# Cross attention outputs turned by DMA instead of TensorE, and the causal mask of nine of twelve self tiles copied by ScalarE

## Time and profile before

| | |
|---|---|
| median of 3 runs | 1791.77 us (1790.55 to 1792.18) |
| profiled execution, own time | 1792.66 us |
| its span | 1791.0 us |
| granted TensorE clock | 0.99 |
| PE busy | 1673.0 us, 93% of the span |
| DVE, ACT, POOL busy | 68%, 62%, 40% |
| one iteration (steady) | 107.1 us |

### The profile page before, as it was taken

The page is one execution under the profiler, slowest core; times in us unless marked ns, Lnnn a source line. Parts: engine busy times, 40 slices in busy tenths (PEclk is TensorE's granted clock), DMA queues, the critical chain, the costliest instruction groups (busy, mean ns, idle before and its releaser), DMA issues.

```text
span 1791.0 us, 34372 instructions
## 1 busy us (share of the span) xinstructions
PE 1673.0 (93%) x12306; PEld 1012.3 (57%) x12306; DVE 1209.0 (68%) x1920; ACT 1102.5 (62%) x1715; POOL 709.2 (40%) x964
## 2 busy tenths in 40 slices
PE   4879999999999999999999999999999999999988
PEld 1445555556555565555656555565655656555655
DVE  4568485685848768485675848668585776848673
ACT  4455665756567465665756567575666756567474
POOL 2251433534334452433534234452433535244320
PEclk9969999999999999999999999999999999999999
DMA  7363342734335363343735335373343635434320
GB/s 184 50 100 50 66 71 38 116 48 77 64 57 86 48 104 60 64 68 45 110 48 81 65 58 81 48 109 58 61 68 49 105 48 84 66 59 65 49 49 13
DMA packets 88720, 124.10 MB, mean 69 GB/s; under 512 B 10577, under 2 KB 56722, under 8 KB 88434
## 3 DMA queue, kind: packets, MB, share of 16 engines
q1 hardware_dynamic: 85570, 114.86, 41.0%
q0 software_dynamic: 2352, 8.26, 1.4%
q10 hardware_dynamic: 768, 0.57, 0.1%
HBM read 21.42 MB, written 8.39 MB: 17 GB/s over the span
## 4 chain that ended last, share of the span: by engine, by line
PE 67%; DVE 9%; POOL 8%; ACT 5%; DMA 5%; issue 5%; ACTq 0%; SPq 0%; DVEq 0%; POOLq 0%
PE o_pair L1392 12%; PE small L1482 8%; DVE negmax L956 6%; PE score L1353 6%; PE small L1223 5%; DMA Q<-negT 4%; PE small L1405 4%; PE small L1239 3%; PE o_pair L1223 3%; PE score L1330 3%; PE small L1516 2%; PE score L1276 2%; POOL q1p L555 2%; POOL q1f L540 2%; PE score L1359 1%
## 5 line engine op out<-in xcount | busy, mean ns | idle before, releaser
L716 ACT ACTIVATE P<-score 128x1024 f32<-128x1024 f32 x448 | 446.9, 1027 | 109.2 <-PE score L1330 50.7
L956 DVE TENSOR_REDUCE negmax<-score 128x4 f32<-128x1024 f32 (+1 forms) x384 | 460.1, 1219 | 29.7 <-PE score L1311 20.4
L978 DVE TENSOR_TENSOR P<-P,cross_bound 128x1024 f32<-128x1024 f32 x192 | 234.0, 1248 | 78.6 <-ACT P L716 78.4
L1392 PE MATMUL o_pair<-P,V 128*32 128x256 f32 (+1 forms) x4096 | 283.1, 363 | 2.4 <-DVE P L978 2.4
L764 ACT ACTIVATE score<-cross_q 128x1024 f32<-128x1024 bf16 x192 | 196.6, 1024 | 45.5 <-DVE negmax L956 44.1
L1353 PE MATMUL score<-Q,K 99*128 99x256 bf16 x1024 | 156.4, 275 | 17.2 <-ACT P L716 16.2
L1392 PEld LDWEIGHTS o_pair<-P,V 128*32 128x32 f32 x4096 | 86.2, 108 | 133.4 <-issue 79.9
L1516 PE MATMUL small<-xnT,w 128*128 128x256 f32 x600 | 156.7, 379 | 0.0
L516 POOL TENSOR_TENSOR x<-x,ffn 128x1024 f32<-128x1024 f32 x15 | 33.0, 2197 | 294.3 <-DVE negmax L956 294.3
L1353 PEld LDWEIGHTS score<-Q,K 99*128 99x128 bf16 x1024 | 84.4, 98 | 108.4 <-ACT P L716 56.2
L1311 PE MATMUL score<-K,Q 96*128 96x256 bf16 x768 | 119.6, 279 | 19.4 <-ACT score L764 15.5
(11 more groups left out here) (192 smaller groups left out, 3222.3 us busy)
## 6 DMA issues: line engine op xcount, KB each, us to landing
K<-k2p SPq DMA_DIRECT2D x96, 256.0 KB, 6.7
Q<-q2p SPq DMA_DIRECT2D x192, 128.0 KB, 4.0
Q<-q1p SPq DMA_DIRECT2D x90, 256.0 KB, 6.0
x_in<-in_x SPq DMA_DIRECT2D x16, 512.0 KB, 5.6
ctxT<-in_ctx SPq DMA_DIRECT2D x16, 512.0 KB, 5.3
k2f<-q1f SPq DMA_DIRECT2D x32, 256.0 KB, 5.3
out_y<-x POOLq DMA_DIRECT2D x15, 512.0 KB, 3.5
K<-k1p SPq DMA_DIRECT2D x90, 64.0 KB, 3.6
```

The lines of the kernel that those rows point to most:

```text
L716: A.activation(P[:, t % 4, :], score[b][:, :, :], ACT.Exp, scale=SCALE).then_inc(score_free[b], 1)
L956: V.tensor_reduce(negmax[:, k, h:h + 1024 // w], s.rearrange("p (h w) -> p h w", w=w), AX.X, ALU.max, negate=True).then_inc(score_free[b], 1)
L978: V.tensor_tensor(p, p, cross_bound[:, t % 2, :].unsqueeze(1).broadcast_to([128, 4, SEQ]), ALU.min).then_inc(probs_masked[1], 1)
L1392: last = T.matmul(o_ps[ob][32 * j:32 * j + 32, SEQ * gg + q0:SEQ * gg + SEQ], v, p, start=s == 0, stop=end, tile_position=(0, 32 * j), ski ...
```

## The change

Five things are changed together.

- **Cross outputs.** V2 gets its values and ones in alternate columns, so the values of an output are in the even rows of `o_sb` and the sums in the odd rows. For each of the four units SP moves 64 even rows into `inT` (128 KB) and one row of sums per head into `sums2` (`put_outputs2`). After row maximum 3 DVE takes the reciprocal of all sums (32 x 256), SP spreads these over 128 partitions by four DMAs from 8 partitions each (`put_inverses2`), POOL multiplies (`over_sums`, two of 128 x 512), and PE's `out2` reads `inT`. PE's `unit_turn` and `heads_turned` for the cross attention, DVE's `normalise` and ACT's two copies of turned outputs go. The final group keeps the old way.
- **Causal mask.** Self tiles take three buffers in turn (`o_pair` is the third). Tiles 0 to 2 keep their mask matmuls; for tiles 3 to 11 ACT copies the mask in first (`self_premask`) and PE waits for that copy.
- **v2.** Both halves are computed in the self scores, the evictions move from DVE to ACT, and the value bias is folded into `bo2` once, ahead of the loop. `out2_0` and `out2_1` stand before and after self tile 11.
- **k2.** The rest of its second half moves from DVE to a copy on ACT (`keys_full`) and a subtraction on POOL (`keys_rest`).
- **SP.** `put_neg(st, 1, 1)` goes ahead of the last parts of q1 and k1 and of the load of x; part 1 of k2 goes behind `put_neg(st, 0, 1)`.

The diff, cut to its core (row lengths as in the source; the hunks stand in the order of the file: banks, SP, POOL, ACT, DVE, PE):

```diff
-    attention = (["k2_0"] + p("m2T_1", "o2t0", "o2t1", "o2t2", "o2t3")
-                 + ["v2_0", "k2_1", "m1T_0"] + p("oT2_0", "oT2_1") + p("out2_0", "out2_1")
-                 + ["v2_1", "m1T_1", "o1t0", "o1t1", "oT1_0", "o1t2"])
+    attention = (["k2_0"] + p("m2T_1") + ["v2_0", "k2_1", "v2_1", "m1T_0"] + p("out2_0", "out2_1")
+                 + ["m1T_1", "o1t0", "o1t1", "oT1_0", "o1t2"])
...
+            def put_outputs2(g, u):
+
+                bank, before = o_bank(1, g, u)
+                b, gp = u // 2, u % 2
+                sp.wait_ge(o_free[bank], before + 1)
+                sp.dma_start(inT[64 * gp:64 * gp + 64, :, SEQ * b:SEQ * b + SEQ],
+                             o_sb[0:128:2, u % 2, :].rearrange("p (c q) -> p c q", c=NC)).then_inc(o2_moved[u % 2], 16)
+                sp.dma_start(sums2[8 * u:8 * u + 8, :], o_sb[1:128:32, u % 2, :]).then_inc(o2_moved[u % 2], 16)
...
+            def put_inverses2(g):
+
+                sp.wait_ge(inverse2_ready, g + 1)
+                for b in range(GB):
+                    for c in range(NC):
+                        sp.dma_start(over_sum[:, c, SEQ * b:SEQ * b + SEQ],
+                                     inverse2[16 * b + c:16 * b + 16:2, :].unsqueeze(1).broadcast_to([8, HD, SEQ])
+                                     ).then_inc(inverse2_moved[b], 16)
...
+                if prev:
+                    put_neg(st, 1, 1)
+                    put_part("q1", 2, i)
+                    put_part("k1", 2, i)
...
                     sp.wait_ge(xn_ready[0], i + 1)
                     sp.wait_ge(x1b_ready, i + 1)
                     sp.dma_start(x_in[:, :, :], x_v[i + 1]).then_inc(x_loaded, 16)
                 if prev:
-                    put_neg(st, 1, 1)
+                    for u in range(UNITS):
+                        put_outputs2(i - 1, u)
+                    put_inverses2(i - 1)
                 put_neg(st, 0, 0)
-                for n in range(2):
+                put_part("k2", 0, i)
+                put_neg(st, 0, 1)
+                for n in range(1, 3):
                     put_part("k2", n, i)
-                put_neg(st, 0, 1)
-                put_part("k2", 2, i)
                 for b in range(GB):
                     for n in range(3):
...
                 if nxt:
                     put_part("k1", 0, i + 1)
-                    for n in range(1, 3):
-                        put_part("q1", n, i + 1)
-                        put_part("k1", n, i + 1)
+                    put_part("q1", 1, i + 1)
+                    put_part("k1", 1, i + 1)
...
+            G.memset(V2[:, :, :, :], 1.0).then_inc(made, 1)
...
+            def over_sums(g, b):
+
+                for n in range(2):
+                    pool.wait_ge(o2_moved[n], 32 * (UNITS // 2) * (g + 1))
+                pool.wait_ge(inverse2_moved[b], 16 * NC * (g + 1))
+                at = slice(SEQ * b, SEQ * b + SEQ)
+                G.tensor_tensor(inT[:, :, at], inT[:, :, at], over_sum[:, :, at], ALU.mult).then_inc(o2_whole, 1)
...
+            def keys_rest(st, g):
+
+                pool.wait_ge(small_free[st.bank("k2_1")], st.this("k2_1"))
+                G.tensor_tensor(k2f[:, 1, :], k2f[:, 1, :], k2p[:, 0, 1, :], ALU.subtract).then_inc(rest1["k2"], 1)
...
                 cut_third(0, i, 0)
                 if nxt:
                     inverse_root(0, i + 1)
-                if prev:
+                keys_rest(st, i)
+                if prev:
+                    for b in range(GB):
+                        over_sums(i - 1, b)
                     add_bias2(i - 1)
...
                 bk = st.bank(f"k2_{c}")
-                act.wait_ge(small_free[bk], st.this(f"k2_{c}"))
+                A.activation(k2f[:, c, :], small[bk][:, :], ACT.Identity,
+                             bias=bk2[:, c:c + 1]).then_inc(small_free[bk], 1)
+
+            def values2(st, r):
+
+                bk = st.bank(f"v2_{r}")
+                act.wait_ge(small_full[bk], st.this(f"v2_{r}"))
+                A.activation(V2[:, 2 * r:2 * r + 2, :, 0:32:2],
+                             small[bk][:, :].rearrange("p (k h n) -> p k h n", k=2, n=HD),
+                             ACT.Copy).then_inc(small_free[bk], 1)
...
+            def keys_second(st, g, c):
+
+                bk = st.bank(f"k2_{c}")
+                if c == 0:
+                    act.wait_ge(small_free[bk], st.this(f"k2_{c}"))
+                else:
+                    act.wait_ge(rest1["k2"], g + 1)
                 A.activation(k2p[:, 1, c, :], k2f[:, c, :], ACT.Copy).then_inc(part2["k2"], 1)
...
-                    if u >= 2:
+                    if u >= 2 and a == 1 and not last:
+                        act.wait_ge(o2_moved[u % 2], 32 * (g * (UNITS // 2) + u // 2))
+                    elif u >= 2:
                         name = f"o{a + 1}t{u - 2}"
                         act.wait_ge(small_full[st.bank(name)], st.before(name) + 1)
                     A.activation(o_sb[:, u % 2, :], o_ps[b], ACT.Copy).then_inc(o_free[b], 1)
...
+            def self_premask(g, t):
+
+                n, before = self_tile(g, t)
+                act.wait_ge(score_free[n], before)
+                if t % 6 < 4:
+                    A.activation(bufs[n][:, :, :].rearrange("p c (j k) -> p (c j) k", j=2),
+                                 causal_q[:, :].unsqueeze(1).broadcast_to([128, 4, SEQ]),
+                                 ACT.Copy).then_inc(masked[n], 1)
+                else:
+                    A.activation(bufs[n][:, :, :].rearrange("p c (j k) -> p (c j) k", j=4),
+                                 causal_q[:, 128:256].unsqueeze(1).broadcast_to([128, 8, 128]),
+                                 ACT.Copy).then_inc(masked[n], 1)
...
+                self_premask(i, 3)
+                self_premask(i, 4)
+                values2(st, 0)
+                self_premask(i, 5)
+                self_premask(i, 6)
+                keys(st, 1)
+                keys_full(st, 1)
+                self_premask(i, 7)
                 cut_first(0, i, 0)
+                self_premask(i, 8)
                 cut_second(0, i, 0)
-                keys(st, 1)
-                keys_second(st, 0)
+                self_premask(i, 9)
+                values2(st, 1)
+                self_premask(i, 10)
                 maxima(st, 0, 0)
-                if prev:
-                    turns(st, "oT2_", inT)
-                keys_second(st, 1)
+                self_premask(i, 11)
+                keys_second(st, i, 0)
+                keys_second(st, i, 1)
                 cut_first(0, i, 1)
                 cut_second(0, i, 1)
...
+                    if t in (9, 13) and i is None:
                         normalise(st, 1, t // 5 - 1, g)
...
-                    if prev and t in (1, 4):
-                        normalise(st, 1, 2 if t == 1 else 3, i - 1)
+                    if prev and t == 3:
+                        for n in range(2):
+                            dve.wait_ge(o2_moved[n], 32 * (UNITS // 2) * i)
+                        V.reciprocal(inverse2[:, :], sums2[:, :]).then_inc(inverse2_ready, 1)
                     if not prev and t == 2:
                         keys_rest(st, i, 0)
-                    if t == 5:
-                        values2(st, 0)
-                    if t == 7:
-                        keys_rest(st, i, 1)
...
-                values2(st, 1)
...
+                    by_pe = t < SELF_PE_MASKED
+                    if not by_pe:
+                        _, use = masked_use("S1", g, t)
+                        pe.wait_ge(masked[n], use + 1)
+                    elif n == 2:
+                        for ob in range(2):
+                            if positive(g * UNITS):
+                                pe.wait_ge(o_free[ob], g * UNITS)
+                    elif positive(before):
                         pe.wait_ge(score_free[n], before)
                     if s < 4:
                         for j in range(4):
...
+                            last = T.matmul(bufs[n][:, j // 2, SEQ * (j % 2):SEQ * (j % 2) + SEQ],
+                                            Q1[0:KROWS, 4 * s + j, SEQ * b + 128:SEQ * b + 256],
+                                            K1[0:KROWS, s, SEQ * b:SEQ * b + SEQ], start=by_pe and j % 2 == 0,
+                                            stop=not by_pe, skip_group_check=True)
...
+                    for c in range(2) if by_pe else ():
+                        last = T.matmul(bufs[n][:, c, :].rearrange("p (h k) -> p h k", h=2)[:, :, 128:256],
+                                        identb[:, :], again(causal_q[:, 128:256], 2), start=False, stop=True,
+                                        skip_group_check=True)
                     last.then_inc(score_full[n], 1)
...
-                    if t == 1 and a == 0:
-                        tokens(st, "v2", ctxT, wv2, 1)
...
-                    if t == TPU[a] * (u + 1) + LAG + 2 and 0 <= u < UNITS - 1 and (a, u) != (0, 2):
```

(54 more changed lines are left out.)

111 lines of the change are left out of this document (60 added, 51 removed).

## The result

The kernel after takes 1873.89 us (median, 1869.23 to 1876.22), the kernel before beside it 1791.97: a ratio of 1.045 [1.044, 1.047]. It is 82 us slower where 42 us faster were forecast, and outside the range.

What follows compares the result with a forecast made beforehand. PE, busy 93% of the span, was taken as the bound, with DVE right behind in the self scores. 3.3 us gained less 0.5 gives 2.8 per iteration, 42 in 15: span 1791.0 to 1749, median forecast 1750 us, range 1722 to 1788.

Steps and rivals of the forecast that it cites:

- Outside: Prologue, iteration 0 and final piece: prologue nothing, at most 1 us; iteration 0 nothing, give or take 2 us.
- The rival on the slower side: Sums' round trip: reciprocal 4.1 and transfer spacing 2.0 us make self attend's tile 8 1.6 us later, 1816 us; chance 0.09.
- The walk of the loop: Timed path from last cross product to self attend's tile 8: 3.3 us gained at tile 6, 2.8 per iteration after allowance.
- After it nothing changes: Behind self attend's tile 6, the 3.3 us gained there was to stay; ACT is next late.
- the allowance: 0.5 us per iteration taken off for a dozen hand-overs counted at 0.1 us or nothing.
- Turns and masks: PE work removed per iteration: masks on nine tiles 2.9 us, unit turns 2.0, turn of all heads 1.1, together 6.0.
- Cross attend: PE-bound stage losing three turns: all later times come 1.5 us earlier; delayed q1 and k1 parts cost nothing.
- Reciprocal: DVE's one reciprocal of 256 elements in the self scores: 1.9 us, bounded by 0.43 and 4.1.
- Idles at tiles 7, 9, 10: Self scores: PE waits 1.4, 0.4 and 1.1 us in the chain of maximum, ACT mask copy and matmuls.
- Narrow transfers: Rival: inverse transfers reading 8 partitions take double, 2.0 us each, delaying POOL's second product; 1782 to 1792 us, chance 0.25.
- The forecast's line for being wrong: Signs: DVE waiting over 1 us for sums, POOL waiting for inverses' transfers, or PE idle over 3 us in self scores.
- The split: Per iteration, masks (2.9 us) and turns (2.0 + 1.1) counted together as 6.0 us of PE work, before waits.

Runs made afterwards that it cites:

- a_pad20: The kernel after with 20 small unused matmuls (40 TensorE instructions) added once ahead of iteration 0: 1765.29 us, ratio 0.984.
- a_pemask: The kernel after with 20 pads and all 12 self tiles masked by TensorE, cross outputs still by transfers: 1750.12 us, ratio 0.976.
- b_pad100: The kernel before with 100 small matmuls (200 TensorE instructions) added ahead of iteration 0: 1841.5 us, ratio 1.027.
- a_order: The kernel after with 20 pads and POOL's first product put ahead of k2's subtraction: 1739.64 us, ratio 0.971.
- a_bias: As a_order, with POOL's bias sums for out2 moved ahead of the first cut of the self maxima: 1746.98 us, ratio 0.975.
- a_bias_mix: As a_bias, with self tiles 7, 9 and 10 masked by TensorE instead of ScalarE: 1733.61 us, ratio 0.967.

## Why the prediction was wrong

**The step that failed** is in "Outside": "Prologue: two matmuls, a 128x256 sum on DVE (0.43 by the earlier trace rows) and a longer memset ... : nothing, at most 1 us", and with it the sum that counts only durations in the loop. What counted was how many instructions stand ahead of the loop: 25 fewer moved its start over a block's edge. a_pad20 gives the price, 1873.9 - 1765.3 = 109 us, or 8.4 us in each of 13 returns. It is a net price: in after the clock falls in the self scores in 3 of the 13 passes, in a_pad20 in 9, which makes up for part of the 9.3 us at the branch. Neither the sum nor a rival of the prediction had a place for where the loop starts. The rival on the slower side named a late inverse transfer and 1816 us; it isn't what happened.

**The walk of the loop** was right in its path and order up to tile 6 of the self attend, and wrong behind it. On a common clock, from self tile 0 (901.79 before, forecast 1.5 earlier; 677.99 in a_pad20):

```
                          before    forecast    a_pad20 at full clock
self attend's tile 0       20.85      21.3           20.48
tile 2                     23.56      22.7           22.28
tile 6                     28.89      27.1           26.73
```

With what the cross attend brings, a_pad20 is 2.4 + 2.2 = 4.6 us ahead at tile 6, where 3.3 were forecast. But the gain per iteration at full clock is 107.1 - 103.6 = 3.5 us: "After it nothing changes" was wrong by 1.1. A tile of the cross scores waits 1.08 us for ScalarE's mask copy where it waited 0.38, and the first tile of the next iteration starts 0.4 us later behind the work before it, with a wait for a negT transfer. The tile before, then both in a_pad20:

```profile
970.05 0.61 PE L1311 MATMUL score<-K,Q 96*128 96x256 bf16 x4 [0.38 <-ACT score L764]
```

```profile
744.79 0.61 PE L1415 MATMUL score<-K,Q 96*128 96x256 bf16 x4 [1.08 <-ACT score L852]
762.22 0.61 PE L1457 MATMUL score<-Q,K 99*128 99x256 bf16 x4 [0.24 <-DMA Q<-negT]
```

So 3.5 us lies near the forecast's 3.3 (2.8 after the allowance) in part by luck: two errors stand against each other. Step by step:

- *Turns and masks:* TensorE's busy time per iteration falls by 103.04 - 97.61 = 5.4 us of 6.0. In a_pemask, with the turns gone and the masks back, it is 99.82: 3.2 us for the turns (3.1 forecast), and so 2.2 for the masks (2.9 forecast).
- *Cross attend:* shorter by 21.81 - (677.99 - 658.63) = 2.4 us, not 1.5; a wait of 1.17 us for ScalarE's exponential at its third tile (884.53 us in the kernel before) is gone as well, which the prediction had no term for.
- *Reciprocal:* 1.73 us by the row of after below, 1.9 forecast. This was the unknown with the widest bounds, and the nearest row's slope gave it.

```profile
L1224 DVE RECIPROCAL inverse<-sums 32x256 f32<-32x256 f32 x15 | 25.9, 1730 | 0.0
```

- *Idles at tiles 7, 9, 10:* 1.07, 0.28, 0.85 against 1.4, 0.4, 1.1; before out2 0.75 against 0.9. Names and order right.
- *Narrow transfers (rival, 0.25):* the condition was half met. In a_pad20 the four are issued from 1001.70 on, each shows eight semaphore updates where out_y's transfer shows sixteen, and the last updates come at 1004.84, 1006.26, 1007.47 and 1008.57: 1.24 us apart, between the 0.98 taken and the rival's 2.0. POOL's second product starts at 1008.9, so no one waits. The Trainium skill, "DMA: Bandwidth & Descriptors" (Why a DMA increments its semaphore by 16 and not by 1), would have eight engines carry such a copy; the eight updates agree, the doubled price, which the prediction took with it, doesn't. (That rival's sum has a slip: 3.3 less 2.9 us leaves 0.4 us per iteration, not 0.7.)
- *What the walk lacked even at its own task:* idle time was priced at its own length. In 9 of 13 iterations the clock fell behind 2.95 us of it, which cost 1.7 more. The forecast's line for being wrong, "more than 3 us of PE idle in the self scores", lies on just that amount, but no term followed from it.
- *The split:* the prediction summed masks (2.9) and turns (3.1) and then took off the waits from both. The runs show that the waits at tiles 7, 9 and 10 go with ScalarE's masks, which are worth 0.3 us at full clock or less than nothing.

With the loop in place the change gives 1765 us: within the range, 15 above the forecast, and 1.6% faster than before.

## What to carry to other kernels

Before timing an edit of a kernel with a long loop, compare the instruction queue's packets on the two pages; if they jump, the time says little of the edit until the loop is moved (here by 40 instructions of padding) or shortened. Removed work is worth what stays removed when the engine next in the chain has been walked, and idle time on TensorE should be priced with the clock behind it. When two gains don't add up, look in the trace for the step that stands behind both, and after each move ask what it brought forward into a transfer.

## What the runs showed of the hardware that was not expected

- A loop of 1653 TensorE instructions runs with no code loads or with nine 16 KB loads per pass, depending on where it starts. Missing, the branch costs 3.0 us idle (b_pad100), or 2.92 + 4.58 (after) when a block's edge follows at once, and there about 1.8 us more for matmuls at the lower clock.
- Fewer instructions can be slower: with 84 fewer in the loop and 25 fewer ahead of it the kernel came out 4.5% slower, and 40 useless ones more took 5.8% off again.
- The clock fell behind the same four waits in 9 iterations and not in 4, with these waits alike to 0.01 us. What decides between them stays open; without one of the waits (a_order) it never fell in 13.
- Two negT transfers with k2's between them: the second took 4.0 to 4.2 us where the first was late and the second early (a_bias), 3.2 to 3.3 where only the first was late (a_order), 3.0 to 3.2 where only the second was early (a_bias_mix). It wasn't tried by moving ScalarE's copy of negT alone.
